# Scores of two heads on the two row halves of the matmul array, in the second and fourth attention layer

## What is computed

```
q = x @ q_w + q_b ;  kv = concat(ctx, x) @ kv_w + kv_b     # k and v interleaved in kv
scores = (q * hd**-0.5) @ (k * hd**-0.5).T + (masked context keys: very negative)
out = softmax(scores) @ v                                   # 256 queries, 512 keys
x = mlp(rmsnorm(x + out @ out_w + out_b)) added to it
```

## Time and profile before

| what | us |
|---|---|
| median of 3 runs (1436.15, 1440.09, 1443.22) | 1440.09 |
| profiled execution | 1436.25 |
| its span | 1434.4 |
| PE, DVE, ACT, POOL busy | 1271.2, 1031.5, 704.2, 516.7 |
| attention of the second layer, first score to last division | 128.8 |
| the same of the fourth layer, 1230.19 to 1358.71 | 128.5 |
| PE in the second layer's projections: 12 groups, 757.19 to 777.87 | 20.7 |
| the 16 value tiles after them, 777.87 to 792.54 | 14.7 |

### The profile page before, as it was taken

The page is one execution under the profiler, slowest core; times in us unless marked ns, Lnnn a source line. Parts: engine busy times, 40 slices in busy tenths (PEclk is TensorE's granted clock), DMA queues, the critical chain, the costliest instruction groups (busy, mean ns, idle before and its releaser), DMA issues. The chain is left out here.

```text
span 1434.4 us, 27763 instructions
## 1 busy us (share of the span) xinstructions
PE 1271.2 (89%) x9018; PEld 1027.9 (72%) x9018; DVE 1031.5 (72%) x2398; ACT 704.2 (49%) x1494; POOL 516.7 (36%) x671
## 2 busy tenths in 40 slices
PE   2799999999699999998699799969599949799969
PEld 2699999999599999997595466558377735456558
DVE  5488788887678888877656688575488866688574
ACT  2366566666356666666522255531266612155541
POOL 2654554444455444442203000030299913000030
PEclk7899999999899999999899799989799989799989
DMA  4111100000211001000205444120750015444110
GB/s 153 30 30 31 31 29 22 29 29 1 93 37 31 24 29 29 29 15 0 92 1 179 83 85 84 29 75 1 209 108 2 3 48 178 84 86 84 30 63 30
DMA packets 73867, 79.87 MB, mean 56 GB/s; under 512 B 7908, under 2 KB 59606, under 8 KB 73258
## 3 DMA queue, kind: packets, MB, share of 16 engines
q1 hardware_dynamic: 72904, 78.55, 20.4%
q10 hardware_dynamic: 866, 0.09, 0.0%
HBM read 60.81 MB, written 17.57 MB: 55 GB/s over the span
## 5 line engine op out<-in xcount | busy, mean ns | idle before, releaser
L1756 DVE TENSOR_REDUCE s_mx<-s_s_ps 128x1 f32<-128x512 f32 x256 | 173.0, 688 | 48.0 <-PE s_s_ps L1827 42.6
L1732 ACT ACTIVATE s_probT<-s_st_ps 128x1024 f32<-128x1024 f32 x128 | 129.1, 1024 | 131.3 <-PE s_st_ps L1848 131.0
L742 ACT ACTIVATE a_prob<-a_s_ps,a_negmax 128x257 f32<-128x257 f32 x256 | 119.0, 476 | 99.3 <-DVE a_negmax L832 99.3
L682 POOL TENSOR_TENSOR x_v_hi<-a_v_sum,x_one 128x512 fp32r<-128x512 f32 x64 | 67.4, 1053 | 262.8 <-DVE a_v_sum L821 262.8
L1827 PE MATMUL s_s_ps<-l_k_st,l_q_st 127*128 127x512 f32 x256 | 127.2, 508 | 16.5 <-PEq L1220 13.0
L1506 POOL TENSOR_SCALAR s_below<-s_masked,s_mx 128x256 f32<-128x256 f32 x256 | 117.8, 480 | 29.4 <-DVE s_mx L1534 28.6
L847 DVE TENSOR_TENSOR a_pT_lo<-a_t_ps,a_pT_hi 128x512 fp32r<-128x512 f32 x128 | 88.2, 689 | 36.8 <-ACT a_pT_hi L755 34.8
L832 DVE TENSOR_REDUCE a_negmax<-a_s_ps 128x2 f32<-128x514 f32 x128 | 86.7, 687 | 32.5 <-PE a_s_ps L894 30.7
L1827 PEld LDWEIGHTS s_s_ps<-l_k_st,l_q_st 127*128 127x128 f32 x256 | 51.9, 204 | 77.6 <-DVE s_mx L1756 40.5
L1712 POOL COPY l_v_st<-l_v_all 128x256 f32<-128x256 f32 (+1 forms) x32 | 12.5, 401 | 257.3 <-PE s_o_ps L1859 197.4
L755 ACT ACTIVATE a_pT_hi<-a_t_ps 128x512 fp32r<-128x512 f32 x128 | 76.6, 598 | 55.8 <-PE a_t_ps L948 52.7
(11 more groups left out here) (230 smaller groups left out, 3968.4 us busy)
## 6 DMA issues: line engine op xcount, KB each, us to landing
l_k_st<-k_stack SPq DMA_DIRECT2D x96, 128.0 KB
l_q_st<-q_stack SPq DMA_DIRECT2D x96, 64.0 KB, 2.2
x_wqk_raw<-L_xattn_wq SPq DMA_DIRECT2D x32, 128.0 KB, 2.2
x_wqk_raw<-L_xattn_wk SPq DMA_DIRECT2D x32, 128.0 KB, 2.2
x_wv_raw<-L_xattn_wv SPq DMA_DIRECT2D x16, 256.0 KB, 3.1
a_wo_raw<-L_xattn_wo SPq DMA_DIRECT2D x16, 256.0 KB, 3.3
k_stack<-p_k_hi SPq DMA_DIRECT2D x4, 1024.0 KB, 4.9
k_stack<-p_k_lo SPq DMA_DIRECT2D x4, 1024.0 KB, 5.8
```

The costliest lines, as they stand in the source:

```text
L742: nc.scalar.activation(prob[:, n % 2, qt, 0:NK], s_ps[:, n % 2, qt, 0:NK], ACT.Exp, bias=negmax[:, n % 2, qt:qt + 1], accum_out=den[:, n % ...
L1732: nc.scalar.activation(probT[:, (s + 2) % U, n], st_ps[:, 2 * (n % 2):2 * (n % 2) + 2].rearrange("p k t -> p (k t)"), ACT.Exp).then_inc(z. ...
L1756: nc.vector.tensor_reduce(mx[:, s, n:n + 1], s_ps[:, n % 2, 0:c.NK], AX.X, ALU.max).then_inc(z.max_done, 1)
```

## The change

The second and fourth layer get new functions pair_projections and pair_attention in place of small_projections and small_attention (deleted with load_stacks). In words:

- Stacks. Two heads share a slot: the even head of a pair has its 48 rows, the mask row and the maximum row at partitions 0 to 49, the odd one at 64 to 113 (HALF is 64). One slot pair holds all four batches of a group of four heads. A unit is two quads (four heads, two batches), loaded by load_unit with eight DMAs: four of them to 16 and four to 32 partitions. Quads go group by group (batch is q mod 4).
- Attention. An S step is one query half of two heads, two products of 512 columns on the two halves into two banks, with one maximum over both (DVE, 128 by 1024); four per quad. An E step is four products of 256 columns, in turns between the halves, into two of three banks, and ACT takes exp of each bank by itself (eight of 128 by 512). The maxima need two transposes of 4 columns (before one of 8) and two row DMAs per quad. The value products stay; values are read in place, so POOL copies nothing. The Fori loops are gone, and the order is new. Outputs and maxima share a bank, so P0 waits for the negated maxima of the round (mx_out).
- Projections. The turn stage is folded in; every product is three fp32r products of split operands; ACT writes the high parts straight from PSUM and DVE the low parts. The value tiles are eight of 512 columns. Stores go in parts, the first heads first, and units 0 and 1 are loaded between them.
- Weights are split a stage ahead: in the first layer's MLP (ACT after its eleventh GELU, then POOL) and in final_norm, where the weight loads now stand ahead of the two rows that its DVE work waits for.
- Buffers: core.xT is replaced by local tiles, the context's parts are kept for the whole program, and the projected output lies over o_all.

```diff
+    def split_high(self, act, loaded, sem):
+        act.wait_ge(loaded, 48)
+        for raw, hi, _ in self.weight_parts():
+            self.nc.scalar.activation(hi, raw, ACT.Copy).then_inc(sem, 1)
+    def split_low(self, pool, sem):
+        for n, (raw, hi, lo) in enumerate(self.weight_parts()):
+            pool.wait_ge(sem, n + 1)
+            self.nc.gpsimd.tensor_tensor(lo, raw, hi.bitcast(F32), ALU.subtract)
...
+                    if n == 10 and next_layer == 1:
+                        core.split_high(act, next_in, next_hi)
...
+def load_unit(c, sp, q_stack, k_stack, q_st, k_st, v, sem):
+    HD, (g, part) = c.HD, divmod(v, 2)
+    bs, slot = slice(2 * part, 2 * part + 2), g % 2
+    for half in range(2):
+        heads, at = slice(4 * g + half, 4 * g + 4, 2), half * c.HALF
+        for rows, src in ((slice(at, at + HD), slice(0, HD)), (slice(at + HD, at + 3 * HD), slice(0, 2 * HD))):
+            sp.dma_start(k_st[rows, slot, :, bs].bitcast(F32).rearrange("r a b n -> r a (b n)"),
+                         k_stack[heads, src, bs].rearrange("a r b n -> r a (b n)")).then_inc(sem, 16)
+        for rows, src in ((slice(at, at + 2 * HD), slice(0, 2 * HD)),
+                          (slice(at + 2 * HD, at + 3 * HD), slice(HD, 2 * HD))):
+            sp.dma_start(q_st[rows, slot, :, bs].bitcast(F32).rearrange("r a b t -> r a (b t)"),
+                         q_stack[heads, src, bs].rearrange("a r b t -> r a (b t)")).then_inc(sem, 16)
+    return 8 * 16
+def pair_projections(core, c, q_stack, k_stack, q_st, k_st, v_st):
...
+                near, far, whole = slice(0, P // 2), slice(P // 2, P), slice(0, P)
+                for is_k, count in ((True, first_k), (False, first_q)):
+                    for part in range(2):
+                        sp.wait_ge((z.qk_hi, z.qk_lo)[part], count)
+                        store(sp, is_k, part, 0, near, z.stored_first)
+                for is_k in (True, False):
+                    for part in range(2):
+                        store(sp, is_k, part, 0, far, z.stored)
+                sp.wait_ge(z.stored_first, 4 * 16)
+                loaded = load_unit(c, sp, q_stack, k_stack, q_st, k_st, 0, z.first_in)
+                load_unit(c, sp, q_stack, k_stack, q_st, k_st, 1, z.second_in)
+                for is_k, count in ((True, first_q + first_k), (False, 2 * first_q)):
+                    for part in range(2):
+                        sp.wait_ge((z.qk_hi, z.qk_lo)[part], count)
+                        store(sp, is_k, part, 1, whole, z.stored)
+                sp.wait_ge(z.rows_in, 6 * 16)
+                sp.wait_ge(z.first_in, loaded)
+                sp.wait_ge(z.second_in, loaded)
+                sp.wait_ge(z.stored, 8 * 16)
...
+                def product(out, left, right, start, stop):
+                    (a_hi, a_lo), (b_hi, b_lo) = left, right
+                    nc.tensor.matmul(out, a_hi, b_hi, start=start, stop=False)
+                    nc.tensor.matmul(out, a_hi, b_lo, start=False, stop=False)
+                    return nc.tensor.matmul(out, a_lo, b_hi, start=False, stop=stop)
...
+    HD, NKT, HALF, NQ = c.HD, c.NKT, c.HALF, c.NQ
+    NS, NE = 4, 8
+    units = c.quads // 2
+    pe_steps = steps("E0 S0 S1 M0 E1 P0 P1 E2 S2 P2 P3 E3 S3 X0")
+    act_steps = steps("E0 E1 E2 E3 E4 E5 O0 E6 E7")
+    dve_steps = steps("M0 S0 S1 S2 S3 X0")
+    def rounds(body):
+        def quad(i):
+            return i if 0 <= i < c.quads else None
+        for i in range(c.quads + 3):
+            body(quad(i), quad(i - 1), quad(i - 2), quad(i - 3))
+    def batch(q):
+        return q // B, q % B
...
+                def load(v):
+                    wait(sp, z.st_done, NE * 2 * (v - 3))
+                    load_unit(c, sp, q_stack, k_stack, q_st, k_st, v, unit_in[v % 4])
+                def body(first, second, third, fourth):
+                    if first == 0:
+                        load(2)
+                        load(3)
+                    if second is not None:
+                        g, b = batch(second)
+                        sp.wait_ge(z.mx_out, second + 1)
+                        for half in range(2):
+                            m = half * HALF + c.MAX_ROW
+                            sp.dma_start(q_st[m:m + 1, g % 2, :, b].bitcast(F32),
+                                         mxT[2 * half:2 * half + 2, second % 2].bitcast(F32)
+                                         ).then_inc(row_in[second % 2], 16)
+                    if first is not None and first >= 4 and first % 2 == 0 and first // 2 + 2 < units:
+                        load(first // 2 + 2)
+                rounds(body)
...
+                            u = NE * third + n
+                            act.wait_ge(z.st_done, u + 1)
+                            wait(act, z.o_done, third - 1)
+                            nc.scalar.activation(probT[:, third % 2, n // 4, n // 2 % 2, n % 2], st_ps[:, u % 3],
+                                                 ACT.Exp, scale=c.scale).then_inc(z.exp_done, 1)
+                        elif kind == "O" and fourth is not None:
+                            act.wait_ge(z.o_done, fourth + 1)
+                            wait(act, z.x_done, fourth)
+                            nc.scalar.activation(oT[:], o_ps, ACT.Copy).then_inc(z.o_out, 1)
+                rounds(body)
...
+                    a, qt = divmod(n, QT)
+                    nc.vector.tensor_reduce(mx[:, i % 2, qt, a::2], s_ps[:, n % 2], AX.X, ALU.max
+                                            ).then_inc(z.max_done, 1)
...
+                        elif kind == "X" and fourth is not None:
+                            outputs(fourth)
+                        elif kind == "M" and second is not None:
+                            dve.wait_ge(z.mx_turned, second + 1)
+                            wait(dve, row_in[second % 2], 32 * (second // 2))
+                            nc.vector.tensor_scalar(mxT[:, second % 2], x_ps[0:4], -1.0, None, ALU.mult
                                                     ).then_inc(z.mx_out, 1)
...
+                def tiles(half, rows, i):
+                    g, b = batch(i)
+                    at = slice(half * HALF, half * HALF + rows)
+                    return q_st[at, g % 2, :, b], k_st[at, g % 2, :, b]
+                def scores(n, i):
+                    g, b = batch(i)
+                    if n == 0 and b % 2 == 0 and i >= B:
+                        v = i // 2
+                        pe.wait_ge(unit_in[v % 4], per_unit * (v // 4 + (v % 4 > 1)))
+                    wait(pe, z.max_done, NS * i + n - 1)
+                    a, qt = n // QT, n % QT
+                    for half in range(2):
+                        q, k = tiles(half, c.MAX_ROW, i)
+                        mm = nc.tensor.matmul(s_ps[:, n % 2, half], q[:, a, qt * P:(qt + 1) * P], k[:, a],
                                               start=True, stop=True)
                     mm.then_inc(z.s_done, 1)
...
+                        pe.wait_ge(row_in[i % 2], 32 * (i // 2 + 1))
+                    u, (a, pair) = NE * i + 2 * n, divmod(n, 2)
+                    wait(pe, z.exp_done, u - 1)
+                    for j in range(2):
+                        for half in range(2):
+                            q, k = tiles(half, c.MAX_ROW + 1, i)
+                            kt = 2 * pair + j
+                            mm = nc.tensor.matmul(st_ps[:, (u + half) % 3, j * S:(j + 1) * S],
+                                                  k[:, a, kt * P:(kt + 1) * P], q[:, a], start=True, stop=True)
+                            if j == 1:
+                                mm.then_inc(z.st_done, 1)
+                def values(kt, i):
+                    g, b = batch(i)
                     if kt == 0:
+                        pe.wait_ge(z.exp_done, NE * (i + 1))
+                        wait(pe, z.x_out, i)
+                        pe.wait_ge(z.mx_out, min(i + 3, c.quads))
                     for j in range(4):
+                        a, half, at = j // 2, j % 2, kt % 2 * S
+                        mm = nc.tensor.matmul(ox_ps[32 * j:32 * j + 32, 0], v_st[:, b, kt, 4 * g + j],
+                                              probT[:, i % 2, a, kt // 2, half, at:at + S],
+                                              start=(kt == 0), stop=(kt == NKT - 1))
                     if kt == NKT - 1:
                         mm.then_inc(z.o_done, 1)
...
+                        elif kind == "M" and second is not None:
+                            pe.wait_ge(z.max_done, NS * (second + 1))
+                            wait(pe, z.x_out, second - 2)
+                            for qt in range(QT):
+                                mm = nc.tensor.transpose(x_ps[0:4, qt * P:(qt + 1) * P], mx[:, second % 2, qt],
+                                                         core.ident[:])
+                            mm.then_inc(z.mx_turned, 1)
...
+        next_in, next_hi = st.sem("next_in"), st.sem("next_hi")
```

(5 more changed lines are left out.)

559 lines of the change are left out of this document (185 added, 374 removed).

## The result

| runs | median us | ratio to before (95% interval) |
|---|---|---|
| before | 1439.62 (4 runs) | |
| after | 1483.01 (1477.09 to 1485.64, 4 runs) | 1.030 (1.027 to 1.033) |

The account below looks back on a forecast made before the run. PE's instruction list was taken as the bound. From 1436.25 us, attention took off 24.8 and projections 9.4, weight splits added 4.5 and 0.5: 1407.0 for the profiled execution, 1411 median; range 1389 to 1433.

Parts of the forecast that it names:

- the part on the projections: Projections: first stores end at 770.3 at 370 GB/s, first score at 794.5 instead of 799.2, 4.7 us gained.
- The round: Attention, one quad: 6.3 us per full round instead of 7.20, bounds 5.9 and 7.2.
- Rival (a): Attention's packed steps: the halves don't overlap, rounds stay at 7.2 us, 1437, no change; chance 0.07.
- Rival (b): Attention on PE: changes of array shape cost more than 0.1, adding 0.6 us per round; 1427; chance 0.12.
- The whole stage: Attention per layer: nineteen rounds in 112.9 us plus a 3.4 us stall, 116.3 against 128.65, a gain of 12.4.
- the stall in round 2: Attention: PE waits for the row of maxima queued behind units 2 and 3; 3.4 us per layer, 0 to 9.
- Rival (d): Attention: holes in PE's work drop the clock to 1.2 GHz, 3.1 us more per round; 1492; chance 0.05.
- the forecast's own signs of being wrong: Attention: rounds at 7, a window below clock 0.9 past its first 15 us, or PE awaiting row DMAs in later rounds.
- Rival (c): Stack loads stay at 128 GB/s: stall 9 instead of 3.4 and stage start 1 late; 1434; chance 0.07.
- E0: Attention's first E step, in round 2: needs quad 0's row of maxima 10.6 us into the stage; row lands at 13.8.
- (e): Attention: heads on halves are cheaper still, DVE alone sets 5.9 us per round, without the stall; 1390; chance 0.05.
- Weight splits: Final norm loses 4.5 us (0 to 7) to POOL subtractions and late gamma and beta rows; first MLP loses 0.5.

Follow-up runs that it names:

- e5: Changed kernel with weights and biases permuted at the split, so stores of eight heads leave 128 partitions with slowest dimension 16; 1431.4 us (0.996).
- e2: Changed kernel with the stores of heads 0 to 3 and 4 to 7 put together, stack layout kept; 1466.2 us (1.020).
- e3: Changed kernel with the E step's loops over j and half swapped, both products of one half issued before the other's; 1483.35 us (1.032).
- e10: e5 with unit 1 loaded at attention start, units 2 and 3 behind rows; transposed maxima in a score bank, P steps single; 1439.4 us.
- e4: Changed kernel with unit 3 loaded behind the first quad's rows of maxima instead of ahead of them; 1468.5 us (1.021).
- e6: Changed kernel with the rows of maxima sent by GpSimd on its own DMA queue instead of SyncE's; 1520.6 us (1.057).
- e13: e5 with unit 1 later, last stores before unit 0's loads, norm rows before weights, and units loaded in halves behind rows of maxima; 1407.4 us (0.979).
- e12: The kernel of e13 without loads in halves, plus idle PE products in the attention's first three rounds; 1412.5 us (0.982).
- e14: e13 with the transposed maxima in the score bank and P steps kept in pairs; 1397.3 us (0.971).

## Why the prediction was wrong

**The step that failed** is in the part on the projections: "3 MB of stores at 370 GB/s end at 770.3". That rate was read from stores whose slowest dimension is 128 channels; the new ones write head by head, 4 or 8 entries, and run at a quarter to a half of the DMA engines. Of the first 3 MB, issued from 761.2 on, 1.9 MB had moved at 783.5 (87 GB/s), and the rest landed beside the loads until 798.4. The second 3 MB, issued from 798.1 on behind the last loads, landed at 822.4 (130 GB/s over these 24.3 us). First score 822.94 instead of 794.5; the stretch of 45.45 and 46.36 us was to lose 4.7 and became 69.93 and 72.80: 29.2 and 31.1 us, 60 of the 70 us by which the profiled execution (1477.1) missed its forecast of 1407.0. Its own bounds for this part went from 12 us gained to 1 lost, since the loads' rate was varied and the stores' was not. e5 changes nothing in that stage but how the stores are laid over engines and partitions (and joins near and far), and gives 51.7 us back, 24.5 and 25.1 of them in the two projections: shown. e2 joins near and far alone and gives 16.8.

**The round** was right: 6.23 measured, 6.3 forecast; E 0.34 (0.36), S 0.32 (0.31), P pair 1.00 (1.00), maximum 1.15 start to start (1.13). Rival (a) falls, by its price and by the starts in e3: the halves overlap, and need not be in turns. Rival (b) falls at this order; e10 has four more changes of shape per round and takes 0.45 us more at full clock, which fits the 0.1 each of the forecast, though its waits differ too.

**The whole stage**: 122.97 and 120.70 instead of 116.3. First, the stall in round 2 was 5.8 and 5.7 us, not 3.4. The mechanism (rows behind units 2 and 3) was right, with e4, but the loads ran at 157 and 172 GB/s and not at 190, which is 1.3 to 2.6 us, and e6 shows that the place in one queue is not what matters. Second, from the first score to the first division went 31.9 and 31.1 us where the forecast's rounds add up to 27.0, at a granted clock of 0.50. The rounds with S steps alone were right, 5.45 and 6.34 (5.4 and 6.1). The next two were forecast at full clock and were not: without a row wait (e13) the first with E steps takes 6.75 (5.8), the first with P steps 8.1 (6.3). For the first of them e12's 5.84 at clock 1.00 in its second layer points to the clock (in its fourth the same round took 6.86 at a mean of 0.69); for the other it is likely and not shown. Third, one round of 8.02. Tail 14.4 against 13.7. With row waits removed by e13, 115.7: the forecast's 112.9 without stall is missed by 3 us, as much as these first rounds cost too much (26.5 against 23.6).

**Rival (d)**, the clock, was put at 0.05 as one that decides for good. In this kernel it comes for some 25 us at the start and 5 us at a time later, and costs a few us per layer; in the traced execution of e10 it did what the rival said, 10.6 us a round. The window that was held against it (15.58 of 20 us busy at 1.00) holds the tail of the attention before and the out-projection, products of 127 and 128 rows, and says nothing of 50-row steps. Two of the forecast's own signs of being wrong came: the window 840 to 860 at 0.69, and PE waiting for rows in later rounds (0.83 and 0.57 us).

**Rival (c)**, slow loads: 157 and 172 GB/s (190 forecast), between the forecast and its 128; the miss of the first score is not from it, as in e5 the same loads stand in a stage of 45.4 us.

**Sums in the forecast**: its 13.8 for the row's landing less the 10.6 at which E0 needs it is 3.2, not 3.4. Rival (a)'s 0.9 us a round over 26 full rounds makes 1434 and not 1437, (e)'s 0.4 a round and no stall 1394 and not 1390. None of this moves the range or the reason of the miss.

**Weight splits**: final norm +3.6 (forecast 4.5): the rows landed 1.2 us late, and DVE's first eight operations took 5.16 instead of 2.67. POOL's first subtraction began at 1194.6, and these operations at 1195.1:

```profile
1195.10 5.16 DVE L1931 TENSOR_SCALAR x_tok<-x_tok,n_mv,n_rstd 128x256 f32<-128x256 f32 x8 [2.95 <-DMA n_b_row<-L_xattn_beta]
```

With the rows first (e13) the subtraction began at 1160.3, when DVE was at the gamma and beta operations; then DVE kept its pace and POOL took 5.87 us for it. In the MLP one subtraction of POOL took 9.22 us instead of 1.55, and it cost nothing on the path: from the first product to the last addition went 47.0 us, as before (47.1; 0.5 more was forecast).

**Left open**: why the clock stays low with a busy PE in the traced execution of e10, and why 64 partitions give half the rate; only sizes were measured. That e14's first rounds still run at 0.50 (clock 0.50 from 795 to 815) was not mended.

## What to carry to other kernels

Before a measured DMA rate is used for a new transfer, compare the outermost dimension of both sides and the number of partitions, not only bytes and engine: the same bytes went at 100, 200 and 400 GB/s here. When a stage ends on a queue, add up that queue's bytes with the lowest rate that its shapes allow, and hold small urgent DMAs ahead of big loads by issuing less, not by another queue. A wait of PE can cost more than its own length: behind waits of 0.8 and 1.1 us the granted clock dropped here, and rounds of 6.23 took 8.0 to 8.3.
